# Attention's product of probabilities and values as three FP32R passes, over groups of two query tiles

## The reference

```python
y = cond_layer_norm(x, cond, s1_w[i], s1_b[i], b1_w[i], b1_b[i])
q = (y @ wq + bq).reshape(N, 4, 128) * 128 ** -0.5
k = (y @ wk + bk).reshape(N, 4, 128)
v = (y @ wv + bv).reshape(N, 4, 128)
scores = einsum('ehd,ehd->eh', q[src], k[dst])          # one per edge
attn = exp(scores - smax[src]) / denom[src]              # softmax over a node's edges
out = segment_sum(attn[:, :, None] * v[dst], src) 
x = x + out.reshape(N, 512) @ wo + bo
```

## Time and profile before

| | |
|---|---|
| median of the runs | 3517.71 us |
| profiled execution: its time, its span | 3515.15 us, 3513.8 us |
| TensorE busy | 3186.8 us (91% of the span), 13432 instructions |
| weight loads busy | 2126.0 us (61%) |
| VectorE, ScalarE, GpSimd busy | 1926.9 (55%), 1417.8 (40%), 1186.4 us (34%) |
| chain that ended last | PE 71%, DVE 14%, ACT 6%, issue 6% |
| of it by line | L136 to L138 33%, L788 10%, L2282 10%, L2267 5% |

### The profile page before, as it was taken

The page is one execution under the profiler, slowest core; times in us unless marked ns, Lnnn a source line. Parts: engine busy times, 40 slices in busy tenths (PEclk is TensorE's granted clock), DMA queues, the critical chain, the costliest instruction groups (busy, mean ns, idle before and its releaser), DMA issues.

```text
span 3513.8 us, 38688 instructions
## 1 busy us (share of the span) xinstructions
PE 3186.8 (91%) x13432; PEld 2126.0 (61%) x13432; DVE 1926.9 (55%) x4296; ACT 1417.8 (40%) x2263; POOL 1186.4 (34%) x1003
## 2 busy tenths in 40 slices
PE   5999898999977788999988999999999999989998
PEld 2333576444742246775456777777777776777767
DVE  6999522887357763245363446544365444754356
ACT  6888632001340023342244553245432554435444
POOL 3666335776367763342000012300132001410022
PEclk8999998999999999999999999999999999999999
DMA  3555433766247763333011001300113001120012
GB/s 85 160 162 161 157 115 103 203 198 183 77 135 211 210 191 103 87 95 114 12 51 42 7 31 44 114 13 7 60 39 95 7 7 61 49 86 7 7 60 72
DMA packets 137266, 318.07 MB, mean 91 GB/s; under 512 B 25380, under 2 KB 43108, under 8 KB 136046
## 3 DMA queue, kind: packets, MB, share of 16 engines
q0 software_dynamic: 53040, 173.84, 17.4%
q1 hardware_dynamic: 82590, 139.10, 12.6%
q10 hardware_dynamic: 1440, 2.62, 0.2%
HBM read 269.50 MB, written 24.84 MB: 84 GB/s over the span
## 4 chain that ended last, share of the span: by engine, by line
PE 71%; DVE 14%; ACT 6%; issue 6%; DVEq 2%; DMA 1%; POOL 1%; SPq 1%; POOLq 0%; ACTq 0%
PE bank L136 11%; PE bank L138 11%; PE bank L137 11%; PE bank L788 10%; PE bank L2282 10%; PE bank L2267 5%; DVE G L909 4%; PE bank L798 3%; PE bank L1983 2%; PE bank L1632 2%; ACT prob L2354 2%; ACT probT L2330 1%; PE bank L766 1%; DVE x_stats L1918 1%; DVE y_tile L1935 1%
## 5 line engine op out<-in xcount | busy, mean ns | idle before, releaser
L788 PE MATMUL bank<-gathered,selector 128*128 128x512 f32 x1326 | 669.1, 619 | 130.6 <-DVE G L909 88.9
L909 DVE TENSOR_TENSOR G<-G,bank 128x512 f32 x663 | 453.7, 684 | 168.6 <-PE bank L788 96.2
L788 PEld LDWEIGHTS bank<-gathered,selector 128*128 128x128 f32 x1326 | 217.2, 194 | 424.4 <-issue 361.2
L2399 DVE CUSTOM_DVE_ANT_0 prob<-bank,count_by_src 128x512 f32<-128x512 f32 (+1 forms) x480 | 258.5, 589 | 316.2 <-PE bank L138 316.2
L2282 PE MATMUL bank<-probT,values_and_heads 128*128 128x512 f32 (+1 forms) x960 | 366.7, 522 | 6.0 <-DVE values_and_heads L2380 6.0
L1297 POOL TENSOR_TENSOR weight_parts<-weight_ring,weight_parts 128x512 fp32r<-128x512 f32 x136 | 199.9, 1471 | 391.5 <-ACT weight_parts L1269 391.5
L2330 ACT COPY probT<-bank 128x512 f32<-128x512 f32 (+1 forms) x480 | 199.0, 488 | 291.7 <-PE bank L2267 291.7
L814 ACT ACTIVATE sign_src<-node_iota_16bit,src_float 128x1280 bf16<-128x1280 f16 x208 | 282.2, 1361 | 50.9 <-PE bank L798 45.0
L775 ACT COPY G<-bank 128x512 f32<-128x512 f32 x160 | 81.3, 659 | 546.2 <-PE bank L766 546.2
L136 PE MATMUL bank<-weight_parts,lhs_parts 128*128 128x512 f32 x680 | 271.7, 400 | 29.4 <-POOL weight_parts L1297 26.6
L1285 DVE TENSOR_TENSOR lhs_parts<-G,lhs_parts 128x640 fp32r<-128x640 f32 x128 | 107.2, 838 | 336.4 <-ACT lhs_parts L1267 336.2
(11 more groups left out here) (272 smaller groups left out, 6225.8 us busy)
## 6 DMA issues: line engine op xcount, KB each, us to landing
weight_ring<-in_L_gnn_basis SPq DMA_DIRECT2D x64, 256.0 KB, 2.7
weight_ring<-in_L_gnn_bases SPq DMA_DIRECT2D x64, 256.0 KB, 2.6
x_L<-x_rows SPq DMA_DIRECT2D x50, 256.0 KB, 4.4
x_rows<-x_L SPq DMA_DIRECT2D x40, 256.0 KB, 2.0
yT_hi<-yT_new_hi SPq DMA_DIRECT2D x4, 2560.0 KB, 10.9
yT_lo<-yT_new_lo SPq DMA_DIRECT2D x4, 2560.0 KB, 10.9
count_rows<-count SPq DMA_DIRECT2D x10, 640.0 KB, 5.6
count_by_dst<-count_rows SPq DMA_DIRECT2D x10, 640.0 KB, 9.4
```

The lines of the kernel that those rows point to most:

```text
L788: pe.matmul(bank[s % banks][:], sel[:, s % SELECTORS, :], xs[:, s % slots, :], start=True, stop=True).then_inc(*multiplied.inc())
L909: dve.tensor_tensor(g, g, bank[s % banks][:], ALU.add).then_inc(*added.inc())
L2399: dve.tensor_tensor_reduce(out=prob[:, s, c:c + width], in0=bank[n][:, 0:width], in1=count[:, t, c:c + width], scale=1.0, scalar=-2.0 * NE ...
```

## The change

The product `values_of` becomes a split one. Each head's V is split by GpSimd (`split_values_of`) into `V_hi` (two heads deep) and `V_lo`, which takes V's own place. The probabilities are split too: ScalarE's copy `move` writes the rounded part (three copies of 512, 512 and 256 columns instead of four) and VectorE's new `move_lo`, behind `invert`, subtracts it from the banks and writes the rest. `turn` waits for `move_lo` of the tile before, a group's first piece waits for `move_lo` and for V's parts.

Groups are of two query tiles, five per head, 256 columns wide. Product and spread sums of a group share a bank, and groups alternate between banks 6 and 7, so a group waits only until the group before the last has left. The pieces are of five key tiles each, one per query tile, at every tile of a head (none of the head before in a block's first head); none stands behind the projections any more, and behind the last head come a half and a whole group. Leaving is spread over tiles 1, 3, 5, 7 and 9.

`probT` has the same size. For the 10 KB of `V_hi` the space that `dynamic_dma_scratch_size` reserves for DMA descriptors is set to 4096 bytes, and two semaphores are shared with others. The diff, cut (left out: the same renaming of `GROUPS` to `QUERY_GROUPS` in five waits, and the two semaphores):

```diff
 GROUPS = -(-NT // 4)
+PER_GROUP = 2
+QUERY_GROUPS = NT // PER_GROUP
+QUERIES = PER_GROUP * P
 PARTS = [(m, n) for m in range(2) for n in range(len(SPANS))]
-PIECES_BEFORE = {0: [(1, 6, NT)], 1: [(2, 0, 4)], 2: [(2, 4, NT)]}
-PIECES = {5: [(0, 0, 3)], 6: [(0, 3, 6)], 7: [(0, 6, 8)], 8: [(0, 8, NT)], 9: [(1, 0, 3)]}
+PIECES_BEFORE = {0: [(3, 5, NT)], 1: [(4, 0, 5)], 2: [(4, 5, NT)]}
+PIECES = {3: [(0, 0, 5)], 4: [(0, 5, NT)], 5: [(1, 0, 5)], 6: [(1, 5, NT)], 7: [(2, 0, 5)], 8: [(2, 5, NT)],
+          9: [(3, 0, 5)]}
 SEEN = [(c, min(512, N - c)) for c in range(0, N, 512)]
 EDGE_INPUTS = ("src", "dst", "edge_type_8", "edge_type_32", "edge_weight", "edge_weight1")
 
@@ -1741,6 +1745,8 @@
...
     stats = M.new("x_stats", [P, NT, 6])
@@ -1753,17 +1759,18 @@
     nmax = M.new("negated_max", [P, 2])
...
     hw_hi = M.new("head_weights_hi", [P, 2, KC, DH], F32R)
...
     mod_raw = M.new("modulation_loaded", [STACKED, 2, D])
     assert M.at <= C.rows_place
     M.at = heads_only = C.rows_place
     prob = M.new("prob", [P, 2, N])
-    PT = M.new("probT", [P, 2, NT, 4 * P])
+    PT = M.new("probT", [P, 2, 2, NT, QUERIES], F32R)
     end_of_heads = M.at
 
     M.at = C.keep2
@@ -1805,7 +1812,7 @@
...
     spread = C.event("row_sums_spread")
...
@@ -1827,7 +1836,7 @@
...
             g = (i * HEADS + h) * NT + t
             if t:
@@ -2262,6 +2268,7 @@
             pe.wait_ge(*exped(g + 1))
             if g:
                 pe.wait_ge(*moved(g))
+                pe.wait_ge(*moved_lo(g))
             for q in range(NT):
...
         def values_of(h, group, a, b):
 
             head = i * HEADS + h
-            G = head * GROUPS + group
-            first, many = 4 * group, min(4, NT - 4 * group)
+            G = head * QUERY_GROUPS + group
+            first, acc = PER_GROUP * group, bank[6 + G % 2]
             if a == 0:
-                pe.wait_ge(*moved(head * NT + first + many))
-                if G:
-                    pe.wait_ge(*left(G))
+                pe.wait_ge(*moved(head * NT + first + PER_GROUP))
+                pe.wait_ge(*moved_lo(head * NT + first + PER_GROUP))
+                pe.wait_ge(*value_parts(head + 1))
+                if G >= 2:
+                    pe.wait_ge(*left(G - 1))
             for q in range(a, b):
                 width = min(P, N - q * P)
-                ins = pe.matmul(bank[6][:, 0:many * P], slots[0:width, 1 + h, q * P:(q + 1) * P],
-                                PT[0:width, G % 2, q, 0:many * P], start=q == 0, stop=q == NT - 1)
+                keys = slice(q * P, (q + 1) * P)
+                ins = split_matmul(pe, acc[:, 0:QUERIES], [V_hi[0:width, h % 2, keys], V_lo[0:width, 1 + h, keys]],
+                                   [PT[0:width, G % 2, part, q, :] for part in range(2)], q == 0, q == NT - 1)
             if b == NT:
-                pe.wait_ge(*inverted(head * NT + first + many))
-                for t in range(many):
-                    ins = pe.transpose(bank[7][:, t * P:(t + 1) * P],
+                pe.wait_ge(*inverted(head * NT + first + PER_GROUP))
+                for t in range(PER_GROUP):
+                    ins = pe.transpose(acc[:, QUERIES + t * P:QUERIES + (t + 1) * P],
                                        rsum[:, h % 2, first + t:first + t + 1].to_broadcast([P, P]), C.ident[:])
...
                         project_on_pe(m, n, yT)
                         if u == 0:
                             turn(h, NT - 1)
-                    values_of(h, 1, 3, 6)
                 else:
                     turn(h, NT - 1)
-                    values_of(h, 1, 3, NT)
-                    values_of(h, 2, 0, NT)
+                    values_of(h, 3, 5, NT)
+                    values_of(h, 4, 0, NT)
+
+        def moves(h, t):
+
+            G, at = (i * HEADS + h) * QUERY_GROUPS + t // PER_GROUP, t % PER_GROUP
+            cols = slice(at * P, (at + 1) * P)
+            return [(bank[3 + b][:, 0:many * P].rearrange("p (q n) -> p q n", n=P),
+                     [PT[:, G % 2, part, 4 * b:4 * b + many, cols] for part in range(2)])
+                    for b, many in ((0, 4), (1, 4), (2, 2))]
 
         def move(h, t):
             head = i * HEADS + h
-            G, s = head * GROUPS + t // 4, t % 4
+            G, at = head * QUERY_GROUPS + t // PER_GROUP, t % PER_GROUP
             act.wait_ge(*turned(head * NT + t + 1))
-            if G >= 2 and s == 0:
+            if G >= 2 and at == 0:
                 act.wait_ge(*attended(G - 1))
-            cols = slice(s * P, (s + 1) * P)
-            for b, many in ((0, 4), (1, 4), (2, 1)):
-                act.copy(PT[:, G % 2, 4 * b:4 * b + many, cols],
-                         bank[3 + b][:, 0:many * P].rearrange("p (q n) -> p q n", n=P))
-            rest = N - (NT - 1) * P
-            act.copy(PT[0:rest, G % 2, NT - 1, cols], bank[5][0:rest, P:2 * P]).then_inc(*moved.inc())
+            for of, (hi, lo) in moves(h, t):
+                ins = act.copy(hi, of)
+            ins.then_inc(*moved.inc())
+
+        def move_lo(h, t):
+            dve.wait_ge(*moved((i * HEADS + h) * NT + t + 1))
+            for of, (hi, lo) in moves(h, t):
+                ins = dve.tensor_tensor(lo, of, hi.bitcast(F32), ALU.subtract)
+            ins.then_inc(*moved_lo.inc())
 
...
         def spread_sums(h, group):
-            G, many = (i * HEADS + h) * GROUPS + group, min(4, NT - 4 * group)
+            G = (i * HEADS + h) * QUERY_GROUPS + group
             act.wait_ge(*attended(G + 1))
             if G:
                 act.wait_ge(*left(G))
-            act.copy(over[:, 0:many * P], bank[7][:, 0:many * P]).then_inc(*spread.inc())
+            act.copy(over[:], bank[6 + G % 2][:, QUERIES:2 * QUERIES]).then_inc(*spread.inc())
+
+        def leaving(t):
+
+            return {1: [(1, 3)], 3: [(1, 4)], 5: [(0, 0)], 7: [(0, 1)], 9: [(0, 2)]}.get(t, [])
...
                 for t in range(NT):
-                    if h and t in (1, 3):
-                        spread_sums(h - 1, 1 if t == 1 else 2)
-                    if t == NT - 1:
-                        spread_sums(h, 0)
+                    for before, group in leaving(t):
+                        if h >= before:
+                            spread_sums(h - before, group)
                     if t:
                         move(h, t - 1)
                     act.wait_ge(*shift(head * NT + t + 1))
...
         def leave(h, group):
-            G = (i * HEADS + h) * GROUPS + group
-            first, many = 4 * group, min(4, NT - 4 * group)
+            G = (i * HEADS + h) * QUERY_GROUPS + group
             dve.wait_ge(*spread(G + 1))
-            dve.tensor_tensor(slots[:, h, first * P:(first + many) * P], bank[6][:, 0:many * P], over[:, 0:many * P],
-                              ALU.mult).then_inc(*left.inc())
+            dve.tensor_tensor(slots[:, h, group * QUERIES:(group + 1) * QUERIES], bank[6 + G % 2][:, 0:QUERIES],
+                              over[:], ALU.mult).then_inc(*left.inc())
...
-                    if h and t in (1, 3):
-                        leave(h - 1, 1 if t == 1 else 2)
-                    if t == NT - 1:
-                        leave(h, 0)
+                    for before, group in leaving(t):
+                        if h >= before:
+                            leave(h - before, group)
                     dve.wait_ge(*scored(g + 1))
...
@@ -2407,14 +2428,17 @@
                                       ALU.mult).then_inc(*shift.inc())
                     if t:
                         invert(h, t - 1)
+                        move_lo(h, t - 1)
                 if h + 1 < HEADS:
                     for u, (m, n) in enumerate(PARTS):
                         project_on_dve(m, n, 6 * (head + 1) + u + 1)
                         if u == 0:
                             invert(h, NT - 1)
+                            move_lo(h, NT - 1)
                 else:
                     invert(h, NT - 1)
-                    for group in range(1, GROUPS):
+                    move_lo(h, NT - 1)
+                    for group in (3, 4):
                         leave(h, group)
 
...
+        def split_values_of(h):
+            head = i * HEADS + h
+            pool.wait_ge(*values_projected(NT * (i + 1)))
+            if head >= 2:
+                pool.wait_ge(*attended(QUERY_GROUPS * (head - 1)))
+            split_weights(slots[:, 1 + h, :], V_hi[:, h % 2, :], V_lo[:, 1 + h, :], value_parts)
+
         def on_pool():
+            split_values_of(0)
             for h in range(1, HEADS):
                 split_queries_keys(i * HEADS + h)
+                split_values_of(h)
...
-    nc = bacc.Bacc("TRN2", target_bir_lowering=False, num_devices=1)
+    nc = bacc.Bacc("TRN2", target_bir_lowering=False, num_devices=1, dynamic_dma_scratch_size=4096)
```

24 lines of the change are left out of this document (14 added, 10 removed).

## The result

The changed kernel takes 3439.81 us (median of four, 3438.88 to 3439.95) beside 3520.32 us for the kernel before in the same comparison. The ratio is 0.977, 95% interval 0.9756 to 0.9783: faster by 80.5 us, beyond the 0.3% that a measurement can tell. The forecast was 3437, a saving of 79 us. The profiled execution of after took 3439.91 us, its span is 3438.6.

What follows compares the result with a forecast made beforehand. TensorE was taken as the bound, the other engines having room. Savings of 0.6 + 9.7 + 4.1 + 5.4 = 19.8 us per block, 79 in four, gave 3436 from 3515.15, 3438 by the median; forecast 3437, range 3420 to 3455.

Steps and rivals of the forecast that it cites:

- A split pass costs 0.117: Values product on TensorE: 150 passes of 256 columns at 0.117 us, 17.5 a head instead of 21.5, 4.0 less.
- rival (d): Values product: split passes don't run as single passes, or a split of V is late; 3507 us, chance 0.03.
- (b): Values product: a 256-column pass takes 0.1075 us, half a 512-column FP32 step; 23 us less, 3414, chance 0.05.
- The order of pieces: TensorE in a head: one five-key-tile piece per tile, 4.58 us or 4.80 at a group's end; 2.55 us of waiting goes.
- The subtraction is hidden, thinly: VectorE's move_lo, taken as 1.79 us, lets the next turn start at T + 4.5; hidden by 0.1 to 0.3 us.
- Rival (a): VectorE's chain becomes the bound: loop of 4.9 us through subtraction, waits and leaving; 3472 us, chance 0.12.
- The head's edge: Scores after the projections wait for the last projected part to be taken: 1.18 us, for three heads a block.
- leaving group 3 delays tile 1, 0.4: Tile 1 of a head: delayed by the leaving of group 3, about 0.4 us in all.
- The sum per block: Attention of one block: 0.6 + 9.7 + 4.1 + 5.4 = 19.8 us saved, 79 in four blocks.
- GpSimd and the descriptor space: GpSimd's split of V per head (about 1.3 + 3.1 us) and the smaller space for gathers: both cost nought.

## Why the prediction was right, point by point

**A split pass costs 0.117.** Right. One tile of after, TensorE's passes of a values piece:

```profile
1894.67 0.28 PE L141 MATMUL bank<-probT,value_parts_hi 128*128 128x256 f32 x1
1894.79 0.28 PE L142 MATMUL bank<-probT,value_parts_lo 128*128 128x256 f32 x1
1894.91 0.28 PE L140 MATMUL bank<-probT,value_parts_hi 128*128 128x256 f32 x1
1895.03 0.28 PE L141 MATMUL bank<-probT,value_parts_hi 128*128 128x256 f32 x1
```

Three steps take 0.36, and over the last group, whose 30 passes run from 2107.89 to 2111.50, one takes 0.120. Probabilities as the moving operand cost what projections do, so the first part of rival (d) falls, and so does (b): by 0.1075 the 30 passes would have taken 3.2 us instead of 3.61.
The Trainium skill's rule that was weighed ("FP8 and Floating Point Precision", TensorE Precision Notes: true FP32 takes four passes) would have given, as an estimate, 5.4 us less work a head, 21.6 a block. The experiment with the plain product gives 12.9 a block for the split, 15.9 with the subtraction's open parts. The rows' 4.0 a head, 16 a block, were right. In the plain kernel a key tile's product takes 2 x (4.98 - 1.09 - 1.73) / 10 = 0.43 us, in split form 3 x 0.117 = 0.35; fifty of them a head differ by 4.0.

**The order of pieces.** Right: with a piece in every tile, turns come 4.58 and 4.79 us apart (4.58 and 4.80 forecast; here tiles 4 to 6), with no wait ahead of them:

```profile
1893.45 1.25 PE L2274 MATMUL bank<-ident,prob 128*128 128x128 f32 x10
1898.03 1.26 PE L2274 MATMUL bank<-ident,prob 128*128 128x128 f32 x10
1902.82 1.26 PE L2274 MATMUL bank<-ident,prob 128*128 128x128 f32 x10
```

**The subtraction is hidden, thinly.** Right. VectorE and ScalarE behind the turn T = 1898.03, in order of time:

```profile
1898.23 0.69 DVE L2420 CUSTOM_DVE_ANT_0 prob<-bank,count_by_src 128x512 f32<-128x512 f32 x1 [0.48 <-PE bank L142]
...
1900.71 1.62 DVE L2352 TENSOR_TENSOR probT<-bank,probT 128x512 fp32r<-128x512 f32 x3 [0.21 <-ACT probT L2346]
1902.29 0.42 DVE L2402 TENSOR_TENSOR values_and_heads<-bank,inverse_sums 128x256 f32<-128x256 f32 x1
1903.01 0.69 DVE L2420 CUSTOM_DVE_ANT_0 prob<-bank,count_by_src 128x512 f32<-128x512 f32 x1 [0.30 <-PE bank L142]
```

```profile
1899.32 1.35 ACT L2346 CAST probT<-bank 128x512 fp32r<-128x512 f32 x3 [1.90 <-PE bank L2274]
1900.55 1.36 ACT L2377 ACTIVATE prob<-prob,negated_max 128x1250 f32<-128x1250 f32 x1
```

The subtraction starts at T + 2.68 (2.65 forecast) and takes 1.62: the lower bound of 1.6, not the 1.79 that was taken. It ends at T + 4.30. Leaving follows at T + 4.26 and is over 0.3 us before the next mask. VectorE is not idle long, but in a tile with a piece it is not what TensorE waits for. How late the next turn can be without cover shows where there is no piece, in the first head:

```profile
1879.60 1.28 PE L2274 MATMUL bank<-ident,prob 128*128 128x128 f32 x10 [1.46 <-DVE probT L2352]
...
1884.07 1.28 PE L2274 MATMUL bank<-ident,prob 128*128 128x128 f32 x10 [1.04 <-DVE probT L2352]
```

4.47 us, forecast 4.5. That the two agree so well is in part luck: the subtraction took 0.17 less than was taken for it, and from its end to the next turn it was 0.15 us (1882.30 + 1.62 to 1884.07), where 0.06 had been allowed. So the cover is 0.11 us in a tile of 4.58 and 0.32 in one of 4.79, which the experiments confirm from both sides: 0.73 us more on VectorE puts it in the open in nearly every tile, and 0.59 us less on TensorE brings the loop to 4.47 and no lower. Rival (a) wanted the loop at 4.9; it is a real bound, 0.11 us away, and not yet the one that decides.

**The head's edge.** The wait ahead of the first scores was read from the earlier trace rows as 1.18 and is 1.17 or 1.18 in every head. The term "leaving group 3 delays tile 1, 0.4" was too large: from projections' end to projections' end two heads take 2054.74 - 1930.16 = 124.58, 62.29 each, where 62.5 was forecast. Of the 62.29, 60.9 are TensorE's work by the forecast's own terms and 1.33 the edge from start to start; 0.1 is left for the leaving and all other waits. One slip changed nothing: by `PIECES`, tiles 3 and 4 of the kernel before had no piece, not tiles 3 to 5.

**The sum per block.** Forecast and measured, in us saved: first head 0.6 and 0.57; second and third head 9.7 and 10.1; last head up to turn 8, 4.1 and 4.3; its end 5.4 and 5.25 (17.73 before, from turn 8 at 2106.67 to the spread sums at 2124.40, and 12.48 after; the forecast took the end of the last product, 2124.56). Together 19.8 and 20.3, which is the whole attention's 267.36 - 247.10. The end in after, TensorE in order of time:

```profile
2099.02 1.26 PE L2274 MATMUL bank<-ident,prob 128*128 128x128 f32 x10
...
2103.46 1.29 PE L2274 MATMUL bank<-ident,prob 128*128 128x128 f32 x10 [1.43 <-DVE probT L2352]
...
2107.89 0.35 PE L140 MATMUL bank<-probT,value_parts_hi 128*128 128x256 f32 x1 [1.15 <-issue]
...
2111.50 0.38 PE L2297 MATMUL bank<-ident,row_sum 128*128 128x128 f32 x2
```

From turn 8 to the spread sums 12.48 us (12.5 forecast), with the two waits that were foreseen: turn 9 at 4.44 behind turn 8 (4.5), the last group at 8.87 (9.0). The profile puts the latter down to "issue", but it is the subtraction's. The last one ends at 2107.79, 0.1 us ahead of the passes:

```profile
2106.17 1.62 DVE L2352 TENSOR_TENSOR probT<-bank,probT 128x512 fp32r<-128x512 f32 x3 [2.60 <-ACT probT L2346]
```

The two kernels without a subtraction (plain FP32, and two passes) have no wait there, while the one with two passes and the subtraction has one of 1.74 us. The 1.49 us of before, for a leaving, did go, but the last group still waits 1.15.

**GpSimd and the descriptor space.** Both cost nought, as forecast. V's first split, GpSimd in order of time:

```profile
1852.88 1.27 POOL L1845 CAST value_parts_hi<-values_and_heads 128x1280 fp32r<-128x1280 f32 x1 [29.86 <-DVE values_and_heads L2186]
1854.23 2.95 POOL L1847 TENSOR_TENSOR value_parts_lo<-values_and_heads,value_parts_hi 128x1280 fp32r<-128x1280 f32 x1
```

1.27 and 2.95 us (1.3 and 3.1 forecast), done at 1857.18, 11 us before the block's first scores and 28 before the first piece at 1885.1. No wait of TensorE names these parts, so the second half of (d) falls. For the space, and the line of after above stand for it, and the experiment of its own, ratio 0.9998.
The Trainium skill, "SBUF — State Buffer", SBUF size, gives that space 16 KiB; a quarter of it carried 663 gathers here at no cost, by that ratio.

**Where the total was lucky.** The forecast of 3437 lies 3 us under the measured median. It came from 79 us saved, measured 80.7 in attention and 1.8 outside it, and from a median of before that a fourth run put 3 us higher. Neither the 0.5 us a block outside attention nor the drift of the stages ahead was in the sum. Whether the 0.5 is the change's isn't shown: with other kernels on other chips these stretches lie between 157.3 and 162.4 us.

## What to carry to other kernels

Before an engine's idle time is filled with a new step, work out the shortest loop from that step back to itself and compare it with the bounding engine's work per turn: here 4.47 against 4.58 us, a cover of 0.11 that made a step of 1.62 us free in every tile with a piece (it still costs 3.0 us a block where there is none and at the end), while 0.73 us more of it cost the whole gain. A reordering and a cheaper form should be priced apart (here 29 and 52 us), and a wait that a block's first turn shows alone, as the 1.18 us at a head's edge, is the price for all turns once the work that covered it has moved; it was worth an edit of its own, and projecting first what is needed in full gave it back. A resource that is made smaller to pay for a change is tested by itself on the kernel before.

## What the runs showed of the hardware

The kernel before takes 3520 us on one chip and 3615 and 3612 on two others, while its attentions on the first and (with the smaller space) the second agree within 0.4 us. Between these two the difference is 93 us at the start of the first attention, and it lies in the gather stages: 30 us in the second aggregation and 63 in the third. The third aggregation as one stretch, first on the first chip, then on the second (the run with the smaller descriptor space, whose ratio on its own chip is 0.9998; columns as in the table of stretches above):

```profile
1020.00:1347.00 327.00, 274.50 (x773) 111.33 (x774) 234.06 (x364) 55.49 (x70) 230.66 (x244) 0.98 0.69 198
```

```profile
1052.00:1442.00 390.00, 295.35 (x776) 122.68 (x777) 234.20 (x363) 56.22 (x71) 230.59 (x244) 0.91 0.58 166
```

The same number of gathers, the same GpSimd, VectorE and ScalarE time, but 390 us instead of 327, and 166 GB/s instead of 198. TensorE's granted clock is lower too, 0.91 against 0.98, in a stretch where it idles more. GpSimd's idle time ahead of the 247 gathers is 153 us instead of 92 there, and 151 in the changed kernel on the third chip. Transfers of gathered rows that take longer on these chips would explain it; no run here separates that from other causes. Two things follow: times of this kernel from different chips can't be compared but by ratio, and where the first attention starts (1953.0 to 1970.5 us on the other chips, one profiled execution of each kernel) can't be read as the effect of an edit, as long as it isn't known what moves it. Attentions are the better measure.

Even the attentions are not free of noise, and it is TensorE's clock. In most attentions and in the stretches between them it falls to its lower level for a few us. The fourth attention of after has a granted clock of 0.88 from 3085.78 to 3100.00, just after TensorE had waited 1.18 us for the last projected part and 1.81 for the first masks; its first two turns are 4.90 us apart. The first attention, with much the same waits, keeps 1.00, and there it is 4.50. That makes most of the 0.5 us by which equal attentions differ. Why one gets it and the other not was not found. Between attentions the clock lies from 0.96 to 0.99, and the longest stretches (162.35 and 161.51 us) are those at 0.96.

The other surprise is small: the subtraction with its sources in a bank and in SBUF runs at 1.62 us for 512, 512 and 256 columns, 0.17 less than the 0.684, 0.684 and 0.424 of the earlier trace rows added up. So successive steps of VectorE overlap, here by as much as the lower bound of the forecast had allowed.
